# A fused embedding, attention and expert kernel: order of scores and maxima, inverse sums by transposes, and splits moved to GpSimd

## The reference

```python
h = tok(x) ++ txt(x_txt)                        # (16, 1101, 128)
n = layernorm(h)
q, k, v = n @ wq, n @ wk, n @ wv                # 8 heads of 64
h = h + concat(softmax(q @ k.T / 8) @ v) @ head_kernel
f = layernorm(h) * ln_scale + ln_bias
h_shared = silu(a) * b                          # a, b = split(f @ shared_in_w.T)
h_expert = silu(c) * d                          # c, d = split(f @ expert_in_w.T)
out = h + h_shared @ shared_out_w.T + shared_out_b
      + sum over experts e of comb[:, e] * (h_expert @ expert_out[e].T + bias[e])
```

## Time and profile before

| | before |
|---|---|
| median of 3 runs | 5006.49 us (5006.3 to 5009.66) |
| profiled execution | 5007.34 us |
| its span | 5005.5 us |
| mean granted TensorE clock | 0.973 |
| TensorE busy | 4551.0 us, 91% |
| VectorE busy | 3373.4 us, 67% |
| GpSimd busy | 2771.3 us, 55% |
| ScalarE busy | 2186.9 us, 44% |

### The profile page before, as it was taken

One profiled execution on the slowest core, in us unless ns is written; L12 is line 12 of the kernel. 1 busy time (PEld: TensorE's weight loads), 2 busy tenths in 40 slices (PEclk: granted clock), 3 DMA queues, 4 the chain that ended last, 5 costly groups with the idle time before them and its releaser, 6 DMA issues.

```text
span 5005.5 us, 89640 instructions
## 1 busy us (share of the span) xinstructions
PE 4551.0 (91%) x32741; PEld 3138.4 (63%) x32741; DVE 3373.4 (67%) x6632; ACT 2186.9 (44%) x5256; POOL 2771.3 (55%) x1609
## 2 busy tenths in 40 slices
PE   5999999999999999999999999998999999999997
PEld 4666666666666666666666666666666666666666
DVE  5667766666666667667676666766666666666765
ACT  2554444444444444444444444444444444444442
POOL 1775555655556555565555655556555565655561
PEclk7999999999999999999999999999999999999998
DMA  1000000000000000000000000000000000000000
GB/s 40 12 6 7 6 16 6 11 7 6 16 6 11 9 13 7 6 11 11 11 7 6 16 6 11 7 6 16 6 10 7 6 16 6 11 7 14 3 1 15
DMA packets 42928, 48.85 MB, mean 10 GB/s; under 512 B 26256, under 2 KB 34311, under 8 KB 42503
## 3 DMA queue, kind: packets, MB, share of 16 engines
q1 hardware_dynamic: 42503, 43.12, 2.8%
HBM read 23.45 MB, written 19.09 MB: 8 GB/s over the span
## 4 chain that ended last, share of the span: by engine, by line
PE 64%; DVE 27%; issue 4%; ACT 2%; SPq 1%; DMA 1%; POOL 0%; DVEq 0%; ACTq 0%; POOLq 0%
PE o_ps L795 20%; PE work L759 16%; DVE part_max L923 10%; PE work L731 8%; DVE h_out L987 4%; PE work L778 4%; PE work L690 3%; PE work L681 2%; PE work L714 2%; PE work L661 2%; PE work L670 2%; DVE sums L1007 2%; DVE heads_t L1017 2%; PE work L720 2%; DVE hid L971 1%
## 5 line engine op out<-in xcount | busy, mean ns | idle before, releaser
L1168 POOL TENSOR_TENSOR sums<-sums,probs 128x736 f32<-128x736 f32 (+3 forms) x1344 | 2369.7, 1763 | 1370.8 <-ACT probs L879 1243.3
L879 ACT ACTIVATE probs<-work 128x368 f32<-128x368 f32 (+3 forms) x3456 | 1419.0, 478 | 1727.1 <-PE work L759 1636.2
L923 DVE TENSOR_REDUCE part_max<-work 128x2 f32<-128x736 f32 (+3 forms) x1474 | 1299.7, 917 | 173.1 <-PE work L778 164.8
L795 PE MATMUL o_ps<-probs,values 128*64 128x368 f32 (+1 forms) x6912 | 1229.2, 492 | 0.4 <-ACT probs L879 0.2
L759 PE MATMUL work<-q_hi,k_hi 64*128 64x368 f32 (+3 forms) x3456 | 683.1, 386 | 198.4 <-DVE part_max L923 98.1
L778 PE MATMUL work<-k_hi,q_hi 64*128 64x368 f32 (+3 forms) x3456 | 654.5, 375 | 149.4 <-DVE part_max L923 112.8
L795 PEld LDWEIGHTS o_ps<-probs,values 128*64 128x64 f32 (+1 forms) x6912 | 458.3, 140 | 528.5 <-issue 398.1
L987 DVE SCALAR_TENSOR_TENSOR h_out<-work,comb,h_out 128x128 f32<-128x128 f32 x1152 | 404.3, 351 | 471.9 <-PE work L731 434.8
L1164 POOL TENSOR_TENSOR sums<-probs 128x736 f32<-128x736 f32 (+1 forms) x192 | 336.4, 1752 | 623.6 <-ACT probs L879 571.1
L759 PEld LDWEIGHTS work<-q_hi,k_hi 64*128 64x128 f32 (+1 forms) x3456 | 334.6, 181 | 459.5 <-issue 199.6
L759 PE MATMUL work<-q_max,k_one 64*128 64x368 f32 (+3 forms) x3456 | 593.2, 330 | 0.0
(11 more groups left out here) (191 smaller groups left out, 5276.1 us busy)
## 6 DMA issues: line engine op xcount, KB each, us to landing
resid_rows<-h_in SPq DMA_DIRECT2D x16, 576.0 KB, 2.8
h_out<-resid_rows SPq DMA_DIRECT2D x16, 576.0 KB, 3.7
h_in<-in_pe_table_dram SPq DMA_DIRECT2D x16, 512.0 KB
out_dram<-h_out SPq DMA_DIRECT2D x16, 512.0 KB
q_max<-max_rows SPq DMA_DIRECT2D x128, 4.0 KB
q_max<-max_rows SPq DMA_DIRECT2D x128, 0.3 KB
counts<-in_x_dram SPq DMA_DIRECT2D x16, 116.0 KB, 2.8
out_raw<-n_expert_out_weight_dram SPq DMA_DIRECT2D x1, 1024.0 KB
```

The costliest lines, as they stand in the source:

```text
L795: mm = nc.tensor.matmul(o_ps[64 * i:64 * i + 64, 0:cw], values[0:n, t, h * DH:(h + 1) * DH], probs[0:n, s % NP, i, 0:cw], start=(t == 0), ...
L879: nc.scalar.activation(probs[0:n, s % NP, i, 0:cw], work[0:n, banks.of[b, ("score", s)][i], 0:cw], ACT.Exp, scale=DH ** -0.5).then_inc(pro ...
L923: nc.vector.tensor_reduce(part_max[0:n, :, j, c:c + 1], work[0:n, ka:ka + 2, 0:keys], AX.X, ALU.max).then_inc(max_taken, 1)
L1168: nc.gpsimd.tensor_tensor(acc, acc, probs[0:n, s % NP, :, 0:cw], ALU.add).then_inc(sums_done, 1)
```

## The change

1. The row phase has the fixed order score, score, maximum, score, maximum, maximum. Maxima are laid three to a group over all 9 groups of the pair before, no longer by `fill`; the row of maxima leaves in the last of them; the projections of a pair are made two pairs ahead, in the last group of a pair. The first score of a pair waits for `q_max` only at its fourth pair of matmuls.
2. The inverse sums: VectorE transposes the 128 x 384 sums from PSUM in blocks of 32 x 32, inverts the 12 columns that hold each sum once, and transposes their broadcast back to rows (`spread`). ScalarE's copy and the four reciprocals go. The sums' matmul has 384 columns; `sums` is set to 1.0 once. The heads' product (`scale`) stays on VectorE, one group after the sum, ahead of the group's units.
3. `flat` is split for all three parts at once in group 7, high part on ScalarE, low part on GpSimd; the low part of `hid` moves from VectorE to GpSimd, behind its additions of the group.
4. The gate is made in group 7 with the choice of the group behind it, the ranking stands behind the maxima of group 8, the weights behind those of group 9. Output projections start in group 0; the statistics stand one group after their tiles, ahead of the units.
5. Experts are ordered by group of experts, then by tile, and VectorE interleaves the last two steps of one with the first two of the next where both are in one group.
6. Inside a group the row's turn comes first and the values last.

```diff
+PADDED = 384
-PROJ = [1, 1, 2, 2, 2, 3, 3, 3, 4]
-STATS, NORMAL, TURN, GATE, WEIGHTS, COUNT = 4, 5, 6, 8, 9, 10
+PROJ = [0, 1, 1, 2, 2, 2, 3, 3, 3]
+STATS, NORMAL, TURN, GATE, COUNT = 4, 5, 6, 7, 10
+CHOOSE, RANK, WEIGHTS = (7, 1), (8, 0), (9, 0)
-MAXROW = 7
+PLACE_V1 = (4, 4, 4, 4, 7, 9, 9, 9, 9)
...
+        mine, g = p >= 1, PAIR * ((p - 1) % PAIRS)
+        if (attn and mine) or (prep and not mine):
+            for n, u in enumerate(maxima(p)):
+                put(g + n // GROUP, u)
+            put(g + PAIR - 1, ("maxrow", p))
+        mine, g = p >= 2, PAIR * ((p - 2) % PAIRS) + PAIR - 1
+        if (attn and mine) or (prep and not mine):
+            for u in projections(p):
+                put(g, u)
...
+            units += [("shared", t) for t in range(3 * c, 3 * c + 3)]
+            units += [("expert", t, g) for g in range(2) for t in range(3 * c, 3 * c + 3)]
...
+    scores = [("score", GROUP * g + i) for i in range(GROUP)] if item.attn else []
+    of = {"S": iter(scores), "M": iter(item.maxima[g])}
+    return [u for kind in "SSMSMM" for u in [next(of[kind], None)] if u]
...
-            elif kind == "sum":
-                q = u[1]
-                cw = CHUNKS[q % NC][1]
-                nc.scalar.copy(sums[:, q % 2, 0, 0:cw], w[:, 0:cw]).then_inc(drained[k], 1)
...
+            if item.post and g == TURN + 1:
+                wait_drained(act, b, *[("turn2", c) for c in range(3)])
+                for c in range(3):
+                    cols = slice(c * GW, (c + 1) * GW)
+                    nc.scalar.copy(flat_hi[:, cols], normed[:, cols]).then_inc(flat_hi_ready, 1)
...
+        def invert(b, q):
+            k = banks.of[b, ("sum", q)][0]
+            n = PAIRS * NC * (b - 1 if q == PAIRS * NC - 1 else b) + q
+            wait_filled(dve, b, ("sum", q))
+            nc.vector.transpose(turned[:], work[:, k, 0:PADDED]).then_inc(drained[k], 1)
+            wait_drained(dve, b, ("sum", q))
+            then(nc.vector.reciprocal(inverse[:], turned[:].rearrange("p (a n) -> p a n", n=32)[:, :, 0]))
+            wait(dve, heads_scaled, n - 1)
+            nc.vector.transpose(spread[:, q % 2, :].rearrange("p (a n) -> p a n", n=32),
+                                inverse[:].unsqueeze(2).broadcast_to((P, PADDED // 32, 32))).then_inc(spread_ready, 1)
...
+        def all_units(b, units):
+            left = []
...
+                for e in range(2):
+                    if left:
+                        add_expert(b, *left.pop(0))
+                    add_expert(b, u, e)
+                for v, e in left:
+                    add_expert(b, v, e)
+                left = [(u, 2), (u, 3)]
...
             for u in item.maxima[g]:
                 maximum(b, u)
+            for u in item.sums[g - 1] if g else []:
+                scale(b, u[1])
             if item.post:
                 for n in range(3):
-                    if g == PROJ[3 * n + 2]:
+                    if g == PROJ[3 * n + 2] + 1:
...
+                gate_chain(b, g, 0)
...
+            for u in item.sums[g]:
+                invert(b, u[1])
+            all_units(b, item.units[g])
+            if item.post:
+                gate_chain(b, g, 1)
...
+        def split_hid(b, c, k2):
+            pool.wait_ge(hid_hi_ready, 3 * KC * (b - 1) + KC * c + k2 + 1)
+            nc.gpsimd.tensor_tensor(hid_lo[:, k2, :], hid[:, 1, k2, :], hid_hi[:, k2, :],
+                                    ALU.subtract).then_inc(hid_split, 1)
```

More of the change, by code:

```diff
@@ L118, in put @@
         if u[0] == "sum":
-            for part in range(DIV):
-                job(g + 1 + part // 2, "invert")
-            job(g + 2, "scale")
+            job(g, "invert")
     def fill(units, first, last, weights):
@@ L171, in plan @@
     for p in range(PAIRS):
[L172 to L177, removed]
+        mine, g = p >= 1, PAIR * ((p - 1) % PAIRS)
[7 more added lines that the diff above has]
+                put(g, u)
     if attn:
-        fill([("v", 1, j) for j in range(NT)], PAIR - 1, 2 * PAIR - 2, EVEN_V)
+        for j, g in enumerate(PLACE_V1):
+            put(g, ("v", 1, j))
     if prep:
@@ L885, in group @@
                 heads(b - 1, PAIRS * NC - 1)
-            for u in item.sums[g]:
-                unit(b, u)
-            if item.post and g == WEIGHTS:
+            if item.post and g == RANK[0]:
                 act.wait_ge(sel_ready, b)
@@ L1010, in divide, with add_expert @@
-        def divide(b, q):
+        def add_expert(b, u, e):
+            _, t, g = u
+            k = banks.of[b, u][0]
+            if e == 0:
+                wait_drained(dve, b, ("expert", t, 0) if g else ("shared", t))
+                wait_filled(dve, b, u)
+            else:
+                dve.wait_ge(s_chain, added[b, u, e - 1])
+            o = h_out[:, t, :]
+            ins = nc.vector.scalar_tensor_tensor(
+                out=o, in0=work[:, k, e * D:(e + 1) * D], scalar=comb[:, t, g * EG + e:g * EG + e + 1],
+                in1=o, op0=ALU.mult, op1=ALU.add)
+            if e == EG - 1:
+                ins.then_inc(drained[k], 1)
+            else:
+                done[0] += 1
+                ins.then_inc(s_chain, 1)
+                added[b, u, e] = done[0]
@@ L1088, in weights, with gate_chain @@
             then(ins)
+        def gate_chain(b, g, late):
+            if (g, late) == CHOOSE:
+                wait_drained(dve, b, ("gate",))
+                choose_group()
+            if (g, late) == RANK:
+                rank_experts()
+            if (g, late) == WEIGHTS:
+                weights(b)
         def group(item, b, g):
@@ L1172, in group @@
                 root(1, b - 1)
[L1173 removed]
+            if item.prep and g == EMBED + 3:
                 root(0, b + 1)
@@ L1177, in group @@
                     add(b, s)
+            if item.post and g == TURN + 1:
+                for c in range(3):
+                    split_flat(b, c)
+            for u in item.units[g - 1] if g else []:
+                if is_last_x(u):
+                    split_hid(b, u[1], u[3])
         for r in range(2):
```

153 lines of the change are left out of this document (62 added, 91 removed).

## The result

The changed kernel takes 4817.23 us (median of four runs, 4815.82 to 4825.35) where the kernel before takes 5008.07 (5006.3 to 5010.81): a ratio of 0.9622, interval 0.9605 to 0.9638. The forecast was 4827 us. Its profiled execution has a span of 4814.3 us.

The account below looks back on a forecast made before the run. TensorE, busy 91% of the span, sets the time, so only its waits can be gained. Terms per steady item sum to -11.35 us, times 15 -170; item 0 and tail 5 each: 5007.3 - 180 = 4827 us, range 4660 to 4950.

Parts of the forecast that it names:

- The row phase: ... 3.17 us.: Head of each of 36 groups: first score to first value matmul takes 3.17 us against 3.80, gaining 22.7 us an item.
- lateness: VectorE not free in time for a group's first reduce: 5 us an item charged, bounds 0 and 12.
- None of it is on the path by itself: VectorE's changed load: worth only in having VectorE free 1.84 us into each group, with no gain of its own.
- VectorE falls by 20-odd us: VectorE's load per item: reciprocals, hid_lo and flat splits removed, transposes added, a net fall of 20-odd us.
- The row arrives at 15.1, TensorE wants it at 10.8: 4.3 us waited.: Gate, group 8: the maxima's row, cast behind a locked ranking, costs 4.3 us once an item, bounds 1.3 and 8.
- A wait of 1.3 us at three pair ends.: Pair ends: TensorE waits 1.3 us for the maxima's row at three an item, bounds 0 and 3.
- What goes with the counts: Weights made in group 9, counts turned in group 10: 2.3 us an item gained; fewer pauses give back 2 of clock.
- Item 0 ... -5. The tail gains some 5: Outside the steady items: item 0's row phases, less pair ends, give -5 us; the tail gains some 5.
- chains that slip between the adds: Rival: VectorE's small steps fit gaps between GpSimd's adds, VectorE in time everywhere; -22.5 us an item, 4660 us, chance 0.19.
- slow transposes: Rival: transposes of 2.0 us make each invert cost more than the reciprocals; 12 x 0.6 us lost, 4930 us, chance 0.07.
- The late VectorE: Rival: scales and gate steps wait for adds, so first reduces start late; at 0.6 us a group 5075 us, chance 0.08.
- if the reduces still start late in groups without gate or statistics: Sign of being wrong, beside an item's pitch above 303 or below 286, or a row wait above 8 us.

Follow-up runs that it names:

- All but the order: The changed kernel with its row phase back in the order score, maximum, score, maximum, score, maximum: 4943.92 us.
- the kernel with both edits: Changed kernel with maxima's row cast before the ranking, flat's low parts heading groups 10 to 12, second head's row loads on ScalarE's queue: 4744.71 us.
- the one that cost 155: The changed kernel with a copy and a reciprocal over all 384 columns in place of the two transposes: 4972.37 us.
- the gate's path: The changed kernel with maxima's row cast before the ranking and flat's low parts made before GpSimd's adds in groups 10 to 12: 4774.09 us.

## Why the prediction was right

The forecast was 180 us, 191 came; the mechanism was as told, and one step was wrong in what it said of VectorE's load.

- *"The row phase: ... 3.17 us."* Three phases of four last 3.15 to 3.45 us, the median is 3.27. What the forecast adds up to an item (its 36 phases at 136.9, less 22.7, plus lateness 5, pair ends 3.9, ranking 4.3, choice 1.6, embedding 1.5, less 0.95 of old row waits) is 129.6 us. Measured: 128.3. The window's own item, 130.7, splits into 36 x 3.25 = 117.0 (the forecast's 114.1 and part of its 5 for lateness), 3.4 at three pair ends, 6.7 in groups 8 and 9, 1.6 in group 23, and 2.0 over the rest. The order alone took the phases from 136.1 to 127.8, and without it they stay at 136.2. What the even spread is worth by itself in this order no run isolates; four to a group gave the same phases.
- *"None of it is on the path by itself"* (VectorE's load). This is the step that failed. Of the load that stands ahead of the units about half is on the path: 21 us more gave 9.5 of pitch, nine more gave six. Load behind the maxima seems to be free: 206 us of it moved away gained none, though GpSimd had to take them. The sum came out right because it was made for the lighter load, for which 5 us of lateness were enough. What was missing is a price for the load's place. In the changed kernel the phases stay at 128.3 only with the short invert and the low part on GpSimd; the kernel before reached 127.8 by the order with its old load, whose reciprocals came in four pieces, so the order doesn't need them everywhere. "VectorE falls by 20-odd us" was wrong too: it fell by 5.5, since the heads' products grew by 9.4 in the lock and the forecast had left that out of the load. The transposes took 0.583 and 0.578 us, 0.05 over the row I took for them. The Trainium skill's page "VectorE: DVE Perf Modes", section "The three transpose paths", has 311 ns for a 128x128 bf16 one, 0.93 for three as an estimate; the one instruction of this trace does 384 fp32 columns in less, and the measurement decides.
- *"The row arrives at 15.1, TensorE wants it at 10.8: 4.3 us waited."* The cast came 10.2 us into group 8, as told, but by luck. The choice of the group was locked as forecast: it took 4.8 us (1568.12 to 1572.96; 1.1 where nothing ran beside it), and the reduce was late by 1.9 where 1.6 were told. The ranking was hardly locked: the late reduces held it back to 1575.81, the last add ended at 1576.45, and it took 2.6 us, not the 4 or more that were to show it. The wait was 2.5 and not 4.3, since TensorE came some 1.5 us later than told and the row 0.3 sooner. Groups 8 and 9 lost 3.0 and 3.7 us over the usual phase: 6.7 where 5.9 were charged, and 5.1 on the mean of the items. In group 8, 1.92 of the 3.0 is the wait for the reduce. The other 1.1 is the clock: from 1568.93 on the score matmuls follow each other at 0.31 us instead of 0.17, the lower level of 1.2 GHz, and that before the wait. TensorE is recorded busy for the whole stretch ahead; 2.18 us of it are the gate's matmuls of 10 columns (L713, from 1565.61). Which of its work lets the clock fall no run isolates, but with the splits before the adds, where the choice isn't locked, group 8 still loses up to 1.1 us to it on the mean. The windows (length; busy PE, PEld, DVE, ACT, POOL; granted clock, DMA share, GB/s):

```profile
1564.00:1568.90 4.90, 4.90 (x41) 3.71 (x39) 3.50 (x5) 1.59 (x4) 4.61 (x4) 1.00 0.00 0
1568.90:1574.00 5.10, 3.25 (x24) 2.41 (x20) 4.96 (x8) 2.52 (x6) 4.96 (x5) 0.67 0.01 2
```

- *"A wait of 1.3 us at three pair ends."* Phases there are 4.33 to 4.41: 1.1 over the usual. The split of the row over two queues takes 0.7 of it away, so it was mostly the row's way through memory.
- *"What goes with the counts"*: 36.5 us of waits fell to 4.1; right. With it the rest fell by 4.7 us an item, where counts, clock and sums had been given 4.0. All but the order has 3.8 of it. Of the clock: stretches at half of it summed to 177 us in the 15 items before and 113 after; at most half of that time is lost, so 5.9 us an item became 3.8, a gain of up to 2.2 where 2 were charged. In the kernel with both edits they are 41 us, so up to 2.4 of its 4.6 us an item are the clock's.
- *"Item 0 ... -5. The tail gains some 5"*: 3.4 and 0.5. Item 0's first residual load came 3.4 us sooner. The 0.25 us a phase did not come: only its first phase got shorter (12.1 to 6.6 us), the others add up to 117.0 us before and 117.1 after. Both terms were too large, together by 6 us, the pitch too small by 1.1 x 15 = 17.
- *The heads' products "will often take 1.5"*: 1.475 at the median. *GpSimd's splits by 0.92*: 1.02.
- Rivals: chains that slip between the adds are out (the choice did not but for one step, nor the chain with four maxima to a group); slow transposes are out at 0.58 us; their price was too low, though: at 2.0 us each the invert would be longer than the one that cost 155. The late VectorE had its mechanism right and too much of it: the reduce came late in group 8, and the waits for all reduces are 43.5 us.
- *Wrong "if the reduces still start late in groups without gate or statistics"*: they hardly do, as long as the invert is short: TensorE waits for them 1.5 us an item in group 8, and in no other group over 0.25.

Left open: why the gate's path and the two queues each gave less than their waits (the two kernels lack 24 and 49 us of what was expected; with the two queues up to 2.0 us an item went to the clock in the rest), and why the scale on GpSimd lengthens the stretches at the lower clock, which make up most of its 37 us.

## What to carry to other kernels

Sum a repeated phase from its first to its last instruction over all its repeats: the table of row phases and rest told at once which part of the change worked where, while TensorE's listed waits miss a good deal of it. Sum the stretches at the lower clock beside it: most of what the scale on GpSimd cost was there, and no wait showed it. Load on a helper engine is to be priced by its place: what stands before the reduce that frees a bank counted here by about a half, what stood behind it brought nothing when it was given to GpSimd. And chains of small steps on VectorE are to be set where GpSimd pauses, with the work that a transfer waits for ahead of them.

## What the hardware showed that was not expected

A chain of small steps with two SBUF inputs on VectorE beside GpSimd lost about a whole GpSimd instruction at a step (0.95, 0.89, 1.04, 1.67 against 0.17 to 0.20 us alone). A step that doesn't wait for the result of the last one can slip through with it, but need not: L1082 took 0.16 us at 1568.99, the second of L1084, which doesn't wait either, 1.04 at 1569.99. The Trainium skill's page "SBUF — State Buffer", section "Who interferes with whom", says that such instructions exclude each other for their full length; the trace agrees for the four long steps, and adds the price by step. A reciprocal costs by its columns, 0.228 us for 12 and 2.553 for 384, so transposing to leave 12 of them pays at 0.58 us a transpose.
